# Cross-attention of a decoder layer: two score banks in place of three, two banks for the softmax sums, stack reads in six DMAs in place of twelve

## The chip, the cores and the metric

The kernel runs on one core of a Trainium2 chip. The metric is the device time of one execution in microseconds (us). The kernel before takes 2713.39 us, the median of three runs.

## The reference

One decoder layer over x of shape 16 x 256 x 512 in fp32: windowed self-attention with rotary embedding (16 heads), a cross-attention, and a mixture in which 16 router columns each pick their top tokens. Only the cross-attention matters here:

```python
def _L0_xattn_ref(q, k, v, gamma):      # q = layernorm(x), k = v = ctx_2048, all (16, 256, 512)
    h = 8                               # heads of 32 rows each
    qh, kh, vh = (t.reshape(B, h, 32, 512) for t in (q, k, v))
    qk = jnp.einsum('bhdq,bhdl->bhql', qh, kh) / sqrt(32)
    sm = jax.nn.softmax(qk, axis=-1)
    ret = jnp.einsum('bhql,bhdl->bhdq', sm, vh)
    return gamma * ret.reshape(B, 256, 512)
x = x + _L0_xattn_ref(_layernorm(x), ctx, ctx, gamma)
```

## The kernel before, in words

Three stages follow each other: self-attention, `cross_attention`, `expert_mix`. The change touches `cross_attention` alone. It works on 32 tiles of 128 rows; a tile holds 4 heads of 32 rows. Each engine has a queue of its own, written out by hand; the engines meet through semaphores only.

Operands are split into a high and a low part (`qp`, `kp`). They are written to DRAM scratch (`sq`, `sk`) and read back as stacks of 96 partitions per head (`qst`, `kst`), so that one matmul sums the products of the parts. `read_stacks` does this on SyncE's queue (SP): two halves of two heads, six DMAs each.

A tile has 4 steps (`c` or `h` = 0 to 3) of 4 turns (`i`, `q`). In a turn TensorE issues:

- `scores`, line 784: for a tile 6 steps ahead, 128 queries x 512 keys into one of three PSUM banks `SC`. VectorE's `maximum` (line 930) reduces the bank to one negated maximum a row (`nmx`). `scores` waits for the maximum three scores back.
- `transposed_scores`, line 793: keys x queries of the present tile, with the row maxima as two further rows, into one of two banks `ST`. ScalarE's `exps` (line 870) turns it into probabilities `prt`. It waits for the exponential two back, and at the first turn of a tile for the maxima's rows.

In turn 1 of each step comes `weigh` (line 804, values times probabilities, four column groups packed), at the end of steps 0 and 2 comes `sums` (line 814, the softmax denominators, of `prt` pairs that GpSimd has added), and in step 2 `max_transposes` (line 821) turns the next tile's maxima into rows. Those go through ScalarE (`mhi`, line 891), VectorE (`mlo`, line 935) and two DMAs of `max_rows` (line 714) into `qst`.

The denominators stand in one bank `SU`. ScalarE takes the logarithm (line 881) and the exponential of its negative (line 885), VectorE makes one Newton step (lines 940 and 945) and multiplies the output (line 952); GpSimd adds the residual (line 758); VectorE takes the statistics (lines 957 and 961). Where these small pieces of work stand among exps and maxima is given by a table `WORK` for each of the two engines: (step, turn), the function, and which tile relative to the present one.

Of the kernel before, what the change touches and what calls it, by code (L numbers as in the profile page):

```python
# [5 lines left out]
F32 = mybir.dt.float32  # L6
# [3 lines left out]
ALU = mybir.AluOpType  # L10
ACT = mybir.ActivationFunctionType
AX = mybir.AxisListType

P = 128
# [3 lines left out]
CB = D // P  # L18
# [574 lines left out]
def cross_attention(nc, x1, ctx_in, ctx_t, gamma, sq, sk, mv2, mv3, x2, cst):  # L593
# [4 lines left out]
    with ctx:  # L598
# [3 lines left out]
        def pb(name):  # L602
            return ctx.enter_context(nc.psum_tensor(name, [P, 512], F32))

        def sem(name):
            return ctx.enter_context(nc.semaphore(name))

        PARTS = 3
        KS = PARTS * XD
        KM = KS + 2  # L610
        AHEAD = 6
        RING = 6
        STACKS = 3
# [11 lines left out]
        qst = [sb(f"qst{i}", [P, XPT, D], F32R) for i in range(STACKS)]  # L625
        kst = [sb(f"kst{i}", [P, XPT, D], F32R) for i in range(STACKS)]
        vt = sb("vt", [P, 3, CB, P], F32)
        prt = [sb(f"xprt{i}", [P, XPT, D], F32) for i in range(RING)]
        nmx = sb("xnmx", [P, 2, XPT * CB], F32)
        mhi = sb("xmhi", [XPT * CB, P], F32R)  # L630
        mlo = sb("xmlo", [XPT * CB, P], F32R)
        ones = sb("xones", [P, XD], F32)
        osb = [sb(f"xosb{i}", [P, D], F32) for i in range(2)]
        rin = sb("xrin", [P, D], F32)
        onm = sb("xonm", [P, D], F32)
        bn = sb("bn3", [P, 6], F32)
        SC = [pb(f"xsc{i}") for i in range(3)]
        ST = [pb(f"xst{i}") for i in range(2)]
        MX = pb("xmx")
        OB = pb("xob")  # L640
        SU = pb("xsu")

        s_shift = sem("x_shift")
        s_gam, s_step = sem("x_gam"), sem("x_step")
# [2 lines left out]
        s_qn, s_qhi, s_qlo = sem("x_qn"), sem("x_qhi"), sem("x_qlo")  # L647
        s_khi, s_klo = sem("x_khi"), sem("x_klo")
        s_qw, s_kw = sem("x_qw"), sem("x_kw")
        s_st = [[sem(f"x_st{i}{k}") for k in range(2)] for i in range(STACKS)]  # L650
        s_row = [sem(f"x_row{i}") for i in range(STACKS)]
        s_ones = sem("x_ones")
        s_sc, s_mx = sem("x_sc"), sem("x_mx")
# [5 lines left out]
        s_log, s_inv, s_new = sem("x_log"), sem("x_inv"), sem("x_new")  # L659
# [11 lines left out]
        @block.sync  # L671
        def _(sp):
            sp.dma_start(gam[:, :], gamma.rearrange("(a b) -> a b", a=1).broadcast_to([P, 1])).then_inc(s_gam, 16)

            def load_x(m):
                sp.dma_start(x2[:, m, :], x1v[m // 2, m % 2]).then_inc(s_xi[m % 6], 16)

            def load_context(m):
                if m >= 4:
                    sp.wait_ge(s_klo, m - 3)  # L680
                sp.dma_start(cin[:, m % 4, :], cv[m]).then_inc(s_ci[m % 4], 16)

            def load_values(m):
                if m >= 3:
                    sp.wait_ge(s_pv, CB * (m - 2))
                sp.dma_start(vt[:, m % 3, :, :], ctx_t[m]).then_inc(s_vt[m % 3], 16)

            def write_queries(m):
                sp.wait_ge(s_qlo, m + 1)
                sp.dma_start(sq[m % 2].rearrange("h p d -> p h d"), qp[m % 2][:, :, :].bitcast(F32)).then_inc(s_qw, 16)  # L690

            def write_keys(m):
                sp.wait_ge(s_klo, m + 1)
                sp.dma_start(sk[m % 2].rearrange("h p d -> p h d"), kp[m % 2][:, :, :].bitcast(F32)).then_inc(s_kw, 16)

            def read_stacks(m):
                sp.wait_ge(s_qw, 16 * m + 16)
                sp.wait_ge(s_kw, 16 * m + 16)
                if m >= STACKS:
                    sp.wait_ge(s_ts, 16 * (m - STACKS) + 16)  # L700
                qv = sq[m % 2].rearrange("h (j r) d -> h r j d", j=XPT)
                kv = sk[m % 2].rearrange("h (j r) d -> h r j d", j=XPT)
                for k in range(2):
                    heads, here = slice(2 * k, 2 * k + 2), s_st[m % STACKS][k]
                    for c in range(PARTS):
                        rows = slice(c, KS, PARTS)
                        sp.dma_start(qst[m % STACKS][rows, heads, :].bitcast(F32), qv[c // 2][:, heads, :]).then_inc(here, 16)
                        sp.dma_start(kst[m % STACKS][rows, heads, :].bitcast(F32), kv[c % 2][:, heads, :]).then_inc(here, 16)

            def max_rows(m):  # L710
                for k, (part, here) in enumerate(((mhi, s_mhi), (mlo, s_mlo))):
                    sp.wait_ge(here, m + 1)
                    row = qst[m % STACKS][KS + k:KS + k + 1, :, :].rearrange("o h (q n) -> o (h q) n", n=P)
                    sp.dma_start(row.bitcast(F32), part[:, :].bitcast(F32)).then_inc(s_row[m % STACKS], 16)

            for m in range(4):
                load_x(m)
                load_context(m)
            load_x(4)
            for n in range(-3, TILES):  # L720
                if tile(n + 2):
                    read_stacks(n + 2)
                if tile(n + 3):
                    write_queries(n + 3)
                    write_keys(n + 3)
                if tile(n + 2):
                    load_values(n + 2)
                if n >= 0 and tile(n + 4):
                    load_context(n + 4)
                if n >= 0 and tile(n + 5):  # L730
                    sp.wait_ge(s_qn, n + 2)
                    load_x(n + 5)
                if tile(n + 1):
                    max_rows(n + 1)
# [42 lines left out]
        def _(pe):  # L777
            def scores(g, q):
                m, h = g // CB, g % CB
                if h % 2 == 0 and q == 0:  # L780
                    pe.wait_ge(s_st[m % STACKS][h // 2], 16 * 2 * PARTS * (m // STACKS + 1))
                if 4 * g + q >= 3:
                    pe.wait_ge(s_mx, 4 * g + q - 2)
                nc.tensor.matmul(SC[(4 * g + q) % 3][:, :], qst[m % STACKS][0:KS, h, q * P:(q + 1) * P],  # L784
                                 kst[m % STACKS][0:KS, h, :], start=True, stop=True).then_inc(s_sc, 1)

            def transposed_scores(s, h):
# [19 lines left out]

            def sums(n, k):
                pe.wait_ge(s_add, XPT * (2 * n + k + 1))
                if k == 0:  # L810
                    pe.wait_ge(s_on, n)
                for h in range(XPT):
                    rows = slice(XD * h, XD * (h + 1))
                    last = nc.tensor.matmul(SU[rows, :], ones[:, :], prt[(CB * n + 2 * k) % RING][:, h, :],
                                            start=(k == 0), stop=(k == 1))
                last.then_inc(s_su, 1)

# [20 lines left out]
        def _(act):  # L838
# [39 lines left out]
            def log_of_sums(n):  # L878
                act.wait_ge(s_su, 2 * n + 2)
                act.wait_ge(s_new, 2 * n)  # L880
                nc.scalar.activation(rin[:, :], SU[:, :], ACT.Ln).then_inc(s_log, 1)

            def inverse_of_sums(n):
                act.wait_ge(s_log, n + 1)
# [2 lines left out]
            def max_round(n):  # L887
                act.wait_ge(s_mt, n + 1)
                if n >= 1:
                    act.wait_ge(s_row[(n - 1) % STACKS], 32 * ((n - 1) // STACKS + 1))  # L890
                nc.scalar.activation(mhi[:, :], MX[0:XPT * CB, 0:P], ACT.Copy).then_inc(s_mhi, 1)

            WORK = {(0, 0): ((k_round, 3),), (0, 2): ((output_evac, -1),), (1, 1): ((normed, 4),), (1, 3): ((q_round, 4),),
                    (2, 2): ((max_round, 1),), (3, 0): ((log_of_sums, -1),), (3, 1): ((inverse_of_sums, -1),)}

            for s in range(FIRST, LAST):
                n, c = s // CB, s % CB
# [8 lines left out]
        def _(dve):  # L906
# [17 lines left out]
            def maximum(g, q):  # L924
                m, h = g // CB, g % CB
                dve.wait_ge(s_sc, 4 * g + q + 1)
                if h == 0 and q == 0 and m >= 2:
                    dve.wait_ge(s_mt, m - 1)
                k = CB * h + q
                nc.vector.tensor_reduce(nmx[:, m % 2, k:k + 1], SC[(4 * g + q) % 3][:, :], AX.X, ALU.max,  # L930
                                        negate=True).then_inc(s_mx, 1)

            def max_rest(n):
# [3 lines left out]

            def newton(n):
                dve.wait_ge(s_inv, n + 1)
                nc.vector.scalar_tensor_tensor(SU[:, :], SU[:, :], -1.0, rin[:, :],  # L940
                                               ALU.mult, ALU.mult).then_inc(s_new, 1)

            def newton_end(n):
                dve.wait_ge(s_new, 2 * n + 1)
                nc.vector.scalar_tensor_tensor(SU[:, :], SU[:, :], 2.0, rin[:, :],
                                               ALU.add, ALU.mult).then_inc(s_new, 1)

            def output(n):
                dve.wait_ge(s_new, 2 * n + 2)
                dve.wait_ge(s_oe, n + 1)  # L950
                dve.wait_ge(s_x2, n)
                nc.vector.tensor_tensor(onm[:, :], osb[n % 2][:, :], SU[:, :], ALU.mult).then_inc(s_on, 1)

            def statistics(n):
                dve.wait_ge(s_x2, n + 1)
# [3 lines left out]
            def mean_and_variance(n):  # L959
                dve.wait_ge(s_bn, 2 * n + 1)  # L960
                nc.vector.bn_aggr(mv3[:, n, :], bn[:, :]).then_inc(s_bn, 1)

            WORK = {(0, 0): ((output, -2),), (0, 2): ((statistics, -3),), (1, 0): ((mean_and_variance, -3),),
                    (2, 2): ((max_rest, 1),), (3, 2): ((newton, -1),), (3, 3): ((newton_end, -1),)}

            for s in range(FIRST, LAST):
                n, c = s // CB, s % CB
# [465 lines left out]
```

## Time and profile before

| | |
|---|---|
| median of 3 runs | 2713.39 us (2711.3 to 2716.83) |
| the profiled execution | 2711.3 us |
| its span, first to last instruction | 2709.6 us |
| TensorE busy in the span | 95% |
| VectorE, ScalarE, GpSimd busy | 66%, 36%, 32% |
| cross-attention's matmuls | from 1979.6 us to about 2505 us of the span |

The profile comes from one execution of its own. "Busy" of TensorE is modelled, since matmuls overlap. A timeline row gives start, duration, engine, line, operation, output and inputs, the count of instructions merged into it, and in brackets the idle time ahead of it with what released it. PEld is the weight load that belongs to a matmul.

### The profile page before, as it was taken

Reading aid. Unit: us, or ns where it says so; the run is one execution under the profiler, and the core shown is the slowest. Engines: PE = TensorE matmul, PEld = TensorE weight load, DVE = VectorE, ACT = ScalarE, POOL = GpSimd, SP = SyncE. Lnnn points to the kernel's source line nnn. Section 1 sums busy time; section 2 is a strip of 40 time slices with the busy share of each in tenths; the row PEclk is TensorE's granted clock in tenths of the full one; section 3 lists DMA queues with packets and bytes.
Section 4 is the critical chain, followed back from the end, with each engine's and each line's share of the span. In section 5 each row is a group of like instructions: output and inputs, shape, how many; then the busy total and the mean of one; then the engine's idle time right before and its main releaser. Section 6 shows DMA issues by size and latency. Waiting matters only on the chain. (4 is left out here: it accounts for less than half of the span.)

```text
span 2709.6 us, 37385 instructions
## 1 busy us (share of the span) xinstructions
PE 2570.5 (95%) x12936; PEld 1916.2 (71%) x12936; DVE 1784.2 (66%) x3705; ACT 967.2 (36%) x2435; POOL 861.6 (32%) x698
## 2 busy tenths in 40 slices
PE   6999999999999999999999999999769999999794
PEld 5788888888888888888888888888634444443683
DVE  5777776565566556556655666666558878876657
ACT  2322223322222332222233222222247777776220
POOL 3211112321112232111123211111148888887000
PEclk9999999999999999999999999999969999999897
DMA  3122233221221222122122212210166676662003
GB/s 117 63 78 94 99 119 117 86 78 63 94 87 70 86 86 78 63 93 95 63 86 86 78 63 87 97 67 32 70 214 216 217 228 211 221 221 74 21 1 124
DMA packets 170153, 280.61 MB, mean 104 GB/s; under 512 B 15089, under 2 KB 81649, under 8 KB 169969
## 3 DMA queue, kind: packets, MB, share of 16 engines
q1 hardware_dynamic: 169968, 278.23, 30.5%
q8 instruction: 107, 1.75, 0.3%
q14 instruction: 78, 0.63, 0.1%
HBM read 185.37 MB, written 92.27 MB: 102 GB/s over the span
## 5 line engine op out<-in xcount | busy, mean ns | idle before, releaser
L324 PE MATMUL pj<-xnt,whi 128*128 128x512 f32 x2048 | 706.7, 407 | 5.5 <-DVE xnt L558 5.5
L417 ACT ACTIVATE pr<-sc,nmx 128x128 f32<-128x128 f32 (+1 forms) x512 | 210.6, 416 | 929.0 <-DVE nmx L503 929.0
L269 POOL TENSOR_TENSOR qt<-rot,swp 128x512 f32<-128x512 f32 x128 | 166.0, 1297 | 1109.6 <-DVE swp L483 1109.6
L324 PEld LDWEIGHTS pj<-xnt,whi 128*128 128x128 f32 x2048 | 387.5, 189 | 98.2 <-DVE xnt L558 6.1
L930 DVE TENSOR_REDUCE xnmx<-xsc 128x1 f32<-128x512 f32 x512 | 333.3, 682 | 105.3 <-PE xsc L784 105.0
L324 PE MATMUL pj<-xnt,wlo 128*128 128x512 f32 x1024 | 400.2, 391 | 0.0
L321 PE MATMUL pj<-whi,xnt 128*128 128x512 f32 x1024 | 352.9, 406 | 4.0 <-issue 4.0
L754 POOL TENSOR_TENSOR xprt<-xprt 128x512 f32<-128x512 f32 x256 | 320.8, 1283 | 72.4 <-PE xob L804 72.4
L870 ACT ACTIVATE xprt<-xst 128x512 f32<-128x512 f32 x512 | 290.7, 595 | 129.3 <-PE xst L793 127.8
L481 DVE TENSOR_TENSOR rot<-pj,trig 128x512 f32<-128x512 f32 x256 | 176.7, 690 | 213.2 <-PE pj L324 213.2
L269 POOL TENSOR_TENSOR kt<-rot,swp 128x512 f32<-128x512 f32 x128 | 164.9, 1288 | 306.6 <-DVE swp L483 306.5
L512 DVE TENSOR_SCALAR pr<-pr,rinv 128x128 f32<-128x128 f32 (+1 forms) x512 | 253.6, 536 | 9.0
L784 PE MATMUL xsc<-kst,qst 96*128 96x512 f32 x512 | 228.2, 453 | 30.3 <-DMA kst<-sk_scratch 30.3
L503 DVE TENSOR_REDUCE nmx<-sc 128x1 f32<-128x128 f32 (+1 forms) x512 | 158.5, 351 | 145.9 <-PE sc L358 141.4
L784 PEld LDWEIGHTS xsc<-kst,qst 96*128 96x128 f32 x512 | 99.7, 195 | 200.2 <-DVE xnmx L930 128.4
L321 PEld LDWEIGHTS pj<-whi,xnt 128*128 128x128 f32 x1024 | 193.4, 189 | 50.3 <-issue 4.3
L793 PE MATMUL xst<-qst,kst 98*128 98x512 f32 x512 | 211.8, 416 | 17.5 <-DMA qst<-xmlo 15.2
L324 PEld LDWEIGHTS pj<-xnt,wlo 128*128 128x128 f32 x1024 | 194.9, 190 | 34.6
L345 PE MATMUL pj<-whi,ohi 128*128 128x512 f32 x512 | 212.5, 415 | 1.4 <-DVE olo L517 1.4
L491 DVE TENSOR_TENSOR xio<-pj,xio 128x512 f32<-128x512 f32 x128 | 88.5, 692 | 180.4 <-PE pj L345 180.4
L345 PE MATMUL pj<-whi,olo 128*128 128x512 f32 x512 | 201.6, 394 | 0.0
L321 PE MATMUL pj<-wlo,xnt 128*128 128x512 f32 x512 | 199.8, 390 | 0.0
(183 smaller groups left out, 4226.1 us busy)
## 6 DMA issues: line engine op xcount, KB each, us to landing
xnt<-xt_scratch SPq DMA_DIRECT2D x48, 1024.0 KB, 7.1
x_scratch<-xio SPq DMA_DIRECT2D x64, 512.0 KB, 3.6
xio<-x_scratch SPq DMA_DIRECT2D x48, 512.0 KB, 4.1
qst<-sq_scratch SPq DMA_DIRECT2D x192, 128.0 KB, 2.5
kst<-sk_scratch SPq DMA_DIRECT2D x192, 128.0 KB, 2.6
raw<-in_w_all_dram SPq DMA_DIRECT2D x64, 256.0 KB, 4.6
xt_scratch<-xnt SPq DMA_DIRECT2D x16, 1024.0 KB, 8.9
sq_scratch<-qp SPq DMA_DIRECT2D x32, 512.0 KB, 3.4
```

Source lines behind the costliest of these rows:

```text
L269: nc.gpsimd.tensor_tensor(qk["QK".index(kind)][h][:, :, :].rearrange("p b n -> p (b n)"), rot[r % 2][:, :], swp[r % 2][:, :], ALU.add).the ...
L321: last = nc.tensor.matmul(bank[:, :], moving[:, i * P:(i + 1) * P], wpart[:, w, :], start=(k == 0), stop=(k == 3 * CB - 1))
L324: last = nc.tensor.matmul(bank[:, :], wpart[:, w, i * HD:(i + 1) * HD], moving, start=(k == 0), stop=(k == 3 * CB - 1))
L345: last = nc.tensor.matmul(PJ[n % 3][:, :], o[:, h, tok], w[:, CH_O + h, :], start=(h == 0 and k == 0), stop=(h == HG - 1 and k == 2))
L417: nc.scalar.activation(pr[:, a % 4, lo:hi], SC[a % 2][:, lo:hi], ACT.Exp, bias=nmx[:, a % 4, t:t + 1], accum_out=rsum[:, a % 4, t:t + 1]). ...
L481: nc.vector.tensor_tensor(ro, bank, table(slice(0, P), q), ALU.mult)
L512: nc.vector.tensor_scalar(pr[:, a % 4, lo:hi], pr[:, a % 4, lo:hi], rinv[:, a % 4, t:t + 1], None, ALU.mult).then_inc(s_pr, 1)
L754: nc.gpsimd.tensor_tensor(a[:, h, :], a[:, h, :], b[:, h, :], ALU.add).then_inc(s_add, 1)
L784: nc.tensor.matmul(SC[(4 * g + q) % 3][:, :], qst[m % STACKS][0:KS, h, q * P:(q + 1) * P], kst[m % STACKS][0:KS, h, :], start=True, stop=T ...
L793: nc.tensor.matmul(ST[h % 2][:, :], kst[n % STACKS][0:KM, h, c * P:(c + 1) * P], qst[n % STACKS][0:KM, h, :], start=True, stop=True).then_ ...
L870: nc.scalar.activation(prt[s % RING][:, h, :], ST[h % 2][:, :], ACT.Exp).then_inc(s_exp, 1)
L930: nc.vector.tensor_reduce(nmx[:, m % 2, k:k + 1], SC[(4 * g + q) % 3][:, :], AX.X, ALU.max, negate=True).then_inc(s_mx, 1)
```

## The change

Of PSUM's eight banks, `SC` has two in place of three and `SU` two in place of one. `scores` waits for the maximum two scores back. `read_stacks` reads all four heads of a part in one DMA: six DMAs of twice the size for a tile, with one semaphore for the whole stack. `sums` of a tile waits for the output of the tile two back. In ScalarE's table the inverse (line 885) goes from turn 1 to turn 2 of step 3. In VectorE's table the two Newton operations leave turns 2 and 3 of step 3 for turns 1 and 3 of step 0 of the next tile, the output goes from (0, 0) to (1, 1), the statistics from (0, 2) to (0, 0), and their aggregation from (1, 0) to (0, 2).

```diff
-        SC = [pb(f"xsc{i}") for i in range(3)]
+        SC = [pb(f"xsc{i}") for i in range(2)]
-        SU = pb("xsu")
+        SU = [pb(f"xsu{i}") for i in range(2)]
...
-        s_st = [[sem(f"x_st{i}{k}") for k in range(2)] for i in range(STACKS)]
+        s_st = [sem(f"x_st{i}") for i in range(STACKS)]
...
-                for k in range(2):
-                    heads, here = slice(2 * k, 2 * k + 2), s_st[m % STACKS][k]
-                    for c in range(PARTS):
-                        rows = slice(c, KS, PARTS)
-                        sp.dma_start(qst[m % STACKS][rows, heads, :].bitcast(F32), qv[c // 2][:, heads, :]).then_inc(here, 16)
-                        sp.dma_start(kst[m % STACKS][rows, heads, :].bitcast(F32), kv[c % 2][:, heads, :]).then_inc(here, 16)
+                for c in range(PARTS):
+                    rows = slice(c, KS, PARTS)
+                    sp.dma_start(qst[m % STACKS][rows, :, :].bitcast(F32), qv[c // 2]).then_inc(s_st[m % STACKS], 16)
+                    sp.dma_start(kst[m % STACKS][rows, :, :].bitcast(F32), kv[c % 2]).then_inc(s_st[m % STACKS], 16)
...
-                if h % 2 == 0 and q == 0:
-                    pe.wait_ge(s_st[m % STACKS][h // 2], 16 * 2 * PARTS * (m // STACKS + 1))
-                if 4 * g + q >= 3:
-                    pe.wait_ge(s_mx, 4 * g + q - 2)
-                nc.tensor.matmul(SC[(4 * g + q) % 3][:, :], qst[m % STACKS][0:KS, h, q * P:(q + 1) * P],
+                if h == 0 and q == 0:
+                    pe.wait_ge(s_st[m % STACKS], 16 * 2 * PARTS * (m // STACKS + 1))
+                if 4 * g + q >= 2:
+                    pe.wait_ge(s_mx, 4 * g + q - 1)
+                nc.tensor.matmul(SC[q % 2][:, :], qst[m % STACKS][0:KS, h, q * P:(q + 1) * P],
...
-                if k == 0:
-                    pe.wait_ge(s_on, n)
+                if k == 0 and n >= 2:
+                    pe.wait_ge(s_on, n - 1)
...
-                    (2, 2): ((max_round, 1),), (3, 0): ((log_of_sums, -1),), (3, 1): ((inverse_of_sums, -1),)}
+                    (2, 2): ((max_round, 1),), (3, 0): ((log_of_sums, -1),), (3, 2): ((inverse_of_sums, -1),)}
...
-            WORK = {(0, 0): ((output, -2),), (0, 2): ((statistics, -3),), (1, 0): ((mean_and_variance, -3),),
-                    (2, 2): ((max_rest, 1),), (3, 2): ((newton, -1),), (3, 3): ((newton_end, -1),)}
+            WORK = {(0, 0): ((statistics, -3),), (0, 1): ((newton, -2),), (0, 2): ((mean_and_variance, -3),),
+                    (0, 3): ((newton_end, -2),), (1, 1): ((output, -2),), (2, 2): ((max_rest, 1),)}
```

## Rows read from the trace of the kernel before

**Rows 1.** Windows: us, busy (x) of PE, PEld, DVE, ACT, POOL; clock, DMA share, GB/s.

```profile
2016.60:2216.70 200.10, 193.87 (x1035) 81.04 (x1033) 158.83 (x273) 152.60 (x293) 172.29 (x138) 1.00 0.69 220
```

**Rows 2.** Timeline of TensorE's matmuls, pieces of one tile, and fifteen tiles later.

```profile
2203.35 0.50 PE L784 MATMUL xsc<-kst,qst 96*128 96x512 f32 x1
2203.69 0.40 PE L793 MATMUL xst<-qst,kst 98*128 98x512 f32 x1
2203.92 0.40 PE L784 MATMUL xsc<-kst,qst 96*128 96x512 f32 x1
2204.16 0.40 PE L793 MATMUL xst<-qst,kst 98*128 98x512 f32 x1
2204.39 0.39 PE L784 MATMUL xsc<-kst,qst 96*128 96x512 f32 x1
2205.44 0.50 PE L793 MATMUL xst<-qst,kst 98*128 98x512 f32 x1 [0.67 <-DMA qst<-xmlo]
...
2207.33 0.50 PE L784 MATMUL xsc<-kst,qst 96*128 96x512 f32 x1
...
2211.57 0.50 PE L784 MATMUL xsc<-kst,qst 96*128 96x512 f32 x1
...
2212.61 0.39 PE L784 MATMUL xsc<-kst,qst 96*128 96x512 f32 x1
2212.99 0.50 PE L793 MATMUL xst<-qst,kst 98*128 98x512 f32 x1
...
2215.01 0.50 PE L784 MATMUL xsc<-kst,qst 96*128 96x512 f32 x1
...
2219.25 0.50 PE L784 MATMUL xsc<-kst,qst 96*128 96x512 f32 x1
...
2441.31 0.47 PE L793 MATMUL xst<-qst,kst 98*128 98x512 f32 x1
```

**Rows 3.** Waits over those fifteen tiles: who waited for whom, us, times, longest.

```profile
PEld xst L793 <- DMA qst<-xmlo: 13.0, 14, 2.3
PEld xst L793 <- ACT xprt L870: 9.1, 30, 0.4
```

**Rows 4.** Timeline of VectorE: first scores of the stage, and a tile's unpacked stretch.

```profile
1980.47 9.66 DVE L930 TENSOR_REDUCE xnmx<-xsc 128x1 f32<-128x512 f32 x16 [14.04 <-PE xsc L784]
...
2212.11 2.48 DVE L930 TENSOR_REDUCE xnmx<-xsc 128x1 f32<-128x512 f32 x4 [0.77 <-PE xsc L784]
```

**Rows 5.** Timeline of TensorE's weight loads at the stage's first scores.

```profile
1979.63 0.93 PEld L784 LDWEIGHTS xsc<-kst,qst 96*128 96x128 f32 x3 [27.51 <-issue]
1981.21 0.29 PEld L784 LDWEIGHTS xsc<-kst,qst 96*128 96x128 f32 x1 [0.65 <-DVE xnmx L930]
```

**Rows 6.** Timeline of ScalarE around the inverse.

```profile
2203.45 0.64 ACT L885 ACTIVATE xrin<-xrin 128x512 f32<-128x512 f32 x1
2204.12 1.08 ACT L870 ACTIVATE xprt<-xst 128x512 f32<-128x512 f32 x2
```

**Rows 7.** Timeline of SyncE's queue: a maxima DMA, first and last stack read.

```profile
2201.26 0.59 SPq L714 DMA_DIRECT2D qst<-xmlo  x1
2204.64 0.61 SPq L707 DMA_DIRECT2D qst<-sq_scratch  x1
...
2211.68 0.60 SPq L708 DMA_DIRECT2D kst<-sk_scratch  x1
```

**Rows 8.** DMA issues from 2100 to 2400 us: count, KB each, median us to landing.

```profile
kst<-sk_scratch SPq DMA_DIRECT2D x114, 128.0 KB, 2.7
...
qst<-xmlo SPq DMA_DIRECT2D x19, 8.0 KB, 3.4
```

**Rows 9.** Windows: the twelve stack reads of one tile, columns as in rows 1.

```profile
2204.60:2212.30 7.70, 7.03 (x39) 2.96 (x39) 6.90 (x13) 5.65 (x11) 5.73 (x6) 1.00 0.57 165
```

**Rows 10.** Timeline of TensorE: second tile's first scores, first transposition of maxima.

```profile
1992.32 1.22 PE L784 MATMUL xsc<-kst,qst 96*128 96x512 f32 x2 [3.14 <-DMA kst<-sk_scratch]
1993.34 0.41 PE L821 MATMUL xmx<-ident,xnmx 128*16 128x128 f32 x1
```

More of the change, by code:

```diff
@@ L809, in sums @@
                 pe.wait_ge(s_add, XPT * (2 * n + k + 1))
-                if k == 0:
-                    pe.wait_ge(s_on, n)
+                if k == 0 and n >= 2:
+                    pe.wait_ge(s_on, n - 1)
                 for h in range(XPT):
                     rows = slice(XD * h, XD * (h + 1))
-                    last = nc.tensor.matmul(SU[rows, :], ones[:, :], prt[(CB * n + 2 * k) % RING][:, h, :],
+                    last = nc.tensor.matmul(SU[n % 2][rows, :], ones[:, :], prt[(CB * n + 2 * k) % RING][:, h, :],
                                             start=(k == 0), stop=(k == 1))
@@ L880, in log_of_sums @@
                 act.wait_ge(s_new, 2 * n)
-                nc.scalar.activation(rin[:, :], SU[:, :], ACT.Ln).then_inc(s_log, 1)
+                nc.scalar.activation(rin[:, :], SU[n % 2][:, :], ACT.Ln).then_inc(s_log, 1)
             def inverse_of_sums(n):
@@ L929, in maximum @@
                 k = CB * h + q
-                nc.vector.tensor_reduce(nmx[:, m % 2, k:k + 1], SC[(4 * g + q) % 3][:, :], AX.X, ALU.max,
+                nc.vector.tensor_reduce(nmx[:, m % 2, k:k + 1], SC[q % 2][:, :], AX.X, ALU.max,
                                         negate=True).then_inc(s_mx, 1)
@@ L939, in newton @@
                 dve.wait_ge(s_inv, n + 1)
-                nc.vector.scalar_tensor_tensor(SU[:, :], SU[:, :], -1.0, rin[:, :],
+                nc.vector.scalar_tensor_tensor(SU[n % 2][:, :], SU[n % 2][:, :], -1.0, rin[:, :],
                                                ALU.mult, ALU.mult).then_inc(s_new, 1)
@@ L944, in newton_end @@
                 dve.wait_ge(s_new, 2 * n + 1)
-                nc.vector.scalar_tensor_tensor(SU[:, :], SU[:, :], 2.0, rin[:, :],
+                nc.vector.scalar_tensor_tensor(SU[n % 2][:, :], SU[n % 2][:, :], 2.0, rin[:, :],
                                                ALU.add, ALU.mult).then_inc(s_new, 1)
@@ L951, in output @@
                 dve.wait_ge(s_x2, n)
-                nc.vector.tensor_tensor(onm[:, :], osb[n % 2][:, :], SU[:, :], ALU.mult).then_inc(s_on, 1)
+                nc.vector.tensor_tensor(onm[:, :], osb[n % 2][:, :], SU[n % 2][:, :], ALU.mult).then_inc(s_on, 1)
             def statistics(n):
```

## The prediction

> **What bounds the kernel now.** The page comes first; it gives the span in which the change touches one stage of three. The windows then show what is tight in it: in 200.1 us TensorE is busy for 193.87 at full granted clock, VectorE for 158.83, ScalarE for 152.60 and GpSimd for 172.29 [rows 1]. So the order of TensorE's queue sets the pace, and everything else matters as far as it makes TensorE wait.
>
> The timeline of one tile shows how [rows 2]. The first transposed score of a tile starts at 2205.44, that of fifteen tiles later at 2441.31: (2441.31 - 2205.44) / 15 = 15.72 us a tile. How much of this is waiting? A score and a transposed score follow each other by 0.23 us (2203.69 to 2203.92), and by 0.34 when the first of them comes after a packed group, since its weight load then can't be hidden (2203.35 to 2203.69). A packed group (`weigh` or `sums`) ends most half-steps. A half-step with its group takes 2.12: 2207.33 to 2211.57 is two of them in 4.24, and 2215.01 to 2219.25 again two in 4.24. In these four, VectorE and ScalarE have the second of the group to catch up. Between lie two stretches in which four scores and four transposed scores follow each other without a group in the middle. I call them A (2211.57 to 2215.01, 3.44 us, with the transposition of maxima) and B (2203.35 to 2207.33, 3.98 us; it runs over a tile's start).
>
> In A one transposed score is 0.38 behind its score in place of 0.23 (2212.61 to 2212.99), and pays 0.11 more for its uncovered load: 0.26 of waiting, and 3.18 without it. In B the tile's first transposed score comes 1.05 after the score (2204.39 to 2205.44), where 0.23 is enough, and again 0.11 for the load: 0.93, and 3.05 without it. A tile without waits is 4 x 2.12 + 3.18 + 3.05 = 14.71 us; so the mean tile waits 15.72 - 14.71 = 1.01, and if A takes its 0.26, B waits 0.75 on average. The waits name the causes: over fifteen tiles 13.0 us for the DMA of `xmlo`, 9.1 for exps [rows 3]. This 1.01 is all that any rearrangement can win while TensorE's work stays.
>
> **The change, part by part.** *Two score banks.* The price is a loop: a score's load, the time until its maximum starts, the maximum, and the release of the bank. Load to maximum is 0.54 at full clock: the score that opens A loads at 2211.57, its maximum starts at 2212.11 [rows 2, 4]. A run of four maxima takes 2.48 and one of sixteen 9.66, so they follow each other by 0.60 and one lasts 0.68 [rows 4]. The release is short: the first maximum ends at 1980.47 + 0.68 = 1981.15, and the load that waited for it starts at 1981.21, 0.06 later [rows 4, 5]. Take A's first load as 0. Its maximum runs from 0.54 to 1.22, and with two banks the third score loads at 1.28. Its matmul stood at 1.04 up to now (2211.57 to 2212.61), with its load hidden. A matmul whose load was held back is followed after 0.34 and not 0.23, so the next one starts at 1.62 in place of 1.27: 0.35 late. The second maximum starts at 1.14 and ends at 1.82, the fourth score loads at 1.88 and is followed at 2.22, where 1.62 + 0.23 + 0.23 = 2.08 would have been its natural time: 0.14 more. So 0.49 in A and, by the same steps, 0.49 in B. In the packed half-steps nothing is lost: the third score there comes 2.12 after the first, and its bank is free at 1.28.
>
> In A these 0.49 take the place of the 0.26 that it waits now, as the exponentials gain the same time. A becomes 3.18 + 0.49 = 3.67.
>
> *VectorE's table.* The five moved operations are the same as before, and cost TensorE nothing as long as VectorE reaches the first maximum of A and B at once. It does: it is idle for 0.77 ahead of A's [rows 4], and in B two Newton operations leave the places where they would now hold a bank. Were they to stay, each 0.60 would come on top in B; without the cover of the following packed group the statistics and the first Newton operation would cost as much. The two `SU` banks only take a wait out of `sums` that was already met; zero, since nothing waits there in the rows.
>
> *The inverse on ScalarE.* It leaves its place ahead of the third exponential of step 3, where it started at 2203.45 while ScalarE waited anyhow [rows 6], for one between the third and the fourth. The third still starts at 2204.12, which is 0.77 after B's first load. A pair of exponentials takes 1.08, so the next operation can follow after 0.48: inverse at 1.25. It lasts 0.64 and, overlapped like the others (0.60 of 0.68 above), lets the fourth exponential start some 0.53 later, at 1.78, and end at 2.38. The tile's second transposed score waits for it, loads at about 2.43, and is followed 0.44 later by the packed group: 2.87. Without this wait it would start at 2.22 and the group at 2.55. So 0.32 more in B; at least nothing (if something else holds B longer), at most the whole 0.53.
>
> *The stack reads.* Twelve issues from 2204.64 to 2211.68 are 0.64 apart [rows 7]; six fewer free SyncE's queue 3.8 us earlier. The transfers of values, context and x that now go out just ahead of the maxima's rows then go out earlier, and the `xmlo` DMA, 3.4 us to landing [rows 8] after its issue at 2201.26 [rows 7], meets an emptier queue. Also B now brings its tile's start 0.35 later. I take the `xmlo` wait as gone: from -0.75 in B, if that were all of it, to 0. So B becomes 3.05 + 0.49 + 0.32 = 3.86.
>
> Against it, the scores of a tile now wait for all of its stack. Bytes: 12 x 128 KB = 1.57 MB. During the stack reads the DMA engines moved 165 GB/s at a share of 0.57 [rows 9], so about 290 at a full share (an estimate); 1.57 MB need 5.4 us. One read lands after 2.7 us [rows 8], of which 128 KB at that rate take 0.45, so the last lands about 2.25 + 5.4 = 7.7 us after the first issue. It is needed at the third score of A. The first issue is 0.48 behind the last transposed score of a tile (2204.16 to 2204.64), thus 1.29 into B; A's third score is at 3.86 + 4.24 + 1.28 = 9.38. That leaves 8.1 - 7.7 = 0.4 us to spare: nothing lost, but narrowly. The Trainium skill, "DMA: Bandwidth & Descriptors", section on the anatomy of one DMA (fitted on GpSimd's path), has about 2.0 us fixed and 436 GB/s after that. By the page the last of six, issued 3.2 us after the first, would land 2.6 us later, at 5.8, with 2.3 us to spare. The row of this kernel shows a slower movement, so the cover is thinner than by the page.
>
> *The start.* Before the first exponential only scores run. The first load to the first maximum takes 1980.47 - 1979.63 = 0.84 at the lower clock [rows 4, 5], so two banks give (0.84 + 0.68 + 0.06) / 2 = 0.79 a score in place of 0.60, and the whole stack is awaited, about 1.4 us longer. Up to the transposition of maxima (1993.34 [rows 10]) that makes 1.4 + 16 x 0.19 = 4.4, of which 3.1 vanish in the wait for the second tile's stack that stands there now [rows 10]: 1.3 late. But six issues fewer are ahead of the maxima's DMAs (-3.8). Between these I take -1.
>
> **The sum.** A tile: 8.48 + 3.67 + 3.86 = 16.01 against 15.72: +0.29, some 30 times +8.7; the start -1. From the profiled execution's 2711.3 us: 2719.0. That execution lies 2.1 us under the median of the runs shown, so 2721 on the median's level.
>
> **The rivals.** *Faster: banks free in time.* If the third score did not really have to wait (a release or a start of the maximum that is 0.3 quicker at this place), only ScalarE's wait stays and the `xmlo` wait is gone: 14.71 + 0.26 + 0.32 = 15.29, 0.43 less a tile, -13 - 1, thus about 2699. It decides at a loop of 1.04 us in place of 1.28. Against it: 0.54, 0.68 and 0.06 are all rows. The skill's "Perfetto Trace Analysis", section on DMA optimizations, holds that larger DMAs use the bandwidth better and may be the main gain. By this rule the change should win at the stack reads, which is this rival's other half; but the stage is not bound by bytes, and the same section says that a split lets some work start sooner.
>
> *No change.* The new waits exist, but of the inverse's 0.32 nothing shows, since the fourth exponential has time, or B's old wait was larger. Then 15.69 a tile and 2711 to 2716 in all.
>
> *Late stacks.* The last read lands more than 0.4 us later than reckoned. Each further microsecond is paid on every tile, because nothing on TensorE overtakes: one microsecond late is +30, thus 2751. For it: rival traffic and issues that took longer; against: the queue is free of other reads then.
>
> *The reorder does nothing and the `xmlo` wait stays.* Then B waits for both, and at most 0.75 x 30 = 22 us come on top: 2743.
>
> **Chances.** Forecast's mechanism 0.58, within it most of the weight over 2719; faster 0.12; no change 0.12; late stacks or a staying `xmlo` wait 0.18. The sum's own error is about 0.1 us a tile, 3 us in all, and a measurement tells about 0.2% (5.4 us) from no change; a part of the forecast's weight, 0.11, thus falls to "within 0.2%". Slower 0.65, same 0.23, faster 0.12. The range reaches from the upper part of the faster side to 1 us of late stacks: 2707 to 2747; the likeliest case alone has 2715 to 2728.
>
> **What would show it.** In the profile after: weight loads of line 784 that wait for `xnmx` inside A and B, about 0.2 to 0.35 us each, twice a stretch; a transposed score at B's end that waits for line 870 with line 885 right ahead of the fourth exponential; no `xmlo` wait of line 793 or a small one; six stack reads 0.64 apart and SyncE's queue idle ahead of `xmhi`; no wait for `kst` or `qst` from scratch at step 2. A tile should measure 16.0 us. The prediction is wrong if loads of line 784 wait for the stack DMAs, if a third score follows its first by 1.04 as now, or if GpSimd's sums hold `sums`.

## Result, and the profile after

The changed kernel takes 2738.35 us, the median of four runs (2734.95 to 2745.65), beside 2714.22 us before: ratio 1.0087, interval 1.0068 to 1.0105. It is slower, by 24 us, inside the range (2707 to 2747), but 17 above the value that I named. The profiled execution took 2744.02 us around a span of 2742.3.

The first lines of the profile's page after (its first transposed score comes 2.7 us later than before, at 2003.28; the rest is in the tiles):

```profile
span 2742.3 us, 37159 instructions
## 1 busy us (share of the span) xinstructions
PE 2591.8 (95%) x12936; PEld 1920.3 (70%) x12936; DVE 1794.3 (65%) x3705; ACT 968.3 (35%) x2435; POOL 861.5 (31%) x698
```

TensorE's timeline after: a stretch B, a stretch A, and the fourth and 31st transposition of maxima:

```profile
2233.70 0.50 PE L782 MATMUL xsc<-kst,qst 96*128 96x512 f32 x1
...
2237.57 0.50 PE L782 MATMUL xsc<-kst,qst 96*128 96x512 f32 x1
...
2241.83 0.50 PE L782 MATMUL xsc<-kst,qst 96*128 96x512 f32 x1
...
2243.82 0.50 PE L782 MATMUL xsc<-kst,qst 96*128 96x512 f32 x1 [0.79 <-DMA kst<-sk_scratch]
...
2246.06 0.50 PE L782 MATMUL xsc<-kst,qst 96*128 96x512 f32 x1
...
2046.53 0.27 PE L819 MATMUL xmx<-ident,xnmx 128*16 128x128 f32 x1
...
2497.55 0.27 PE L819 MATMUL xmx<-ident,xnmx 128*16 128x128 f32 x1
```

A tile takes (2497.55 - 2046.53) / 27 = 16.70 us; by the same two rows of the kernel before (2039.65 and 2465.07) it was 15.76. The two packed half-steps from 2237.57 to 2241.83 still take 4.26. B is 3.87 here, and 3.86 on average over the tiles, against 3.78. A is 4.23 here and 4.34 on average, against 3.44. So nearly all of the 0.95 us a tile is in A. (All averages of this kind are counted over the whole stage's timeline, of which a few rows are shown. Averages of A and B here and below are taken over the stage's 31 tiles without the first three and last two, from one score after a packed group to the next.)

The weight loads say what held them:

```profile
2234.98 0.19 PEld L782 LDWEIGHTS xsc<-kst,qst 96*128 96x128 f32 x1 [0.51 <-DVE xnmx L928]
...
2235.58 0.19 PEld L782 LDWEIGHTS xsc<-kst,qst 96*128 96x128 f32 x1 [0.20 <-DVE xnmx L928]
2236.13 0.19 PEld L791 LDWEIGHTS xst<-qst,kst 98*128 98x128 f32 x1 [0.37 <-ACT xprt L868]
...
2243.82 0.19 PEld L782 LDWEIGHTS xsc<-kst,qst 96*128 96x128 f32 x1 [1.22 <-DMA kst<-sk_scratch]
```

In B the third score loads at 1.28 after the first (2233.70 to 2234.98), the fourth at 1.88, and the second transposed score at 2.43: to the hundredth where the prediction had them. In A the third score waits for the stack and loads at 1.99, 0.71 late; A is only 0.58 longer than 3.65, as the wait of the fourth score is then covered.

The waits over the stage, from 2010 to 2480 us, and the DMA issues from 2100 to 2400:

```profile
PEld xsc L782 <- DMA kst<-sk_scratch: 32.4, 27, 2.7
...
PE xsc L782 <- DMA kst<-sk_scratch: 20.5, 26, 2.3
...
PEld xst L791 <- ACT xprt L868: 9.8, 27, 0.4
```

```profile
qst<-sq_scratch SPq DMA_DIRECT2D x54, 256.0 KB, 4.1
kst<-sk_scratch SPq DMA_DIRECT2D x54, 256.0 KB, 4.7
sq_scratch<-qp SPq DMA_DIRECT2D x18, 512.0 KB, 6.2
...
qst<-xmlo SPq DMA_DIRECT2D x17, 8.0 KB, 1.9
```

No wait for `xmlo` is left, and its DMA lands in 1.9 us where it took 3.4 [rows 8]. In its place stands a wait for `kst` on nearly every tile. SyncE's queue shows why `xmlo` has a free way, and when the reads went out:

```profile
2235.01 0.61 SPq L705 DMA_DIRECT2D qst<-sq_scratch  x1
...
2238.23 0.60 SPq L706 DMA_DIRECT2D kst<-sk_scratch  x1
...
2242.64 0.62 SPq L676 DMA_DIRECT2D x<-x_scratch  x1
2247.60 0.56 SPq L712 DMA_DIRECT2D qst<-xmhi  x1
```

From 2243.3 to 2247.6 the queue is idle. The last stack read is usable at 2243.82, 8.81 us after the first issue at 2235.01. The prediction had 7.7, and 8.1 as the moment from which it costs.

The medians of 4.1 and 4.7 us to landing hide an order. Over the stage the first of a tile's six reads lands in 3.3 us (median), the next in 3.8, 4.2, 4.7 and 5.1, and the sixth, issued 3.22 us after the first, in 5.5.

One thing more is in A. On two of the 25 tiles whose records are complete, the granted clock fell after the wait (see e3), and there A is 7.30 and 6.23; on the other 23 it is 4.11. So of the 0.69 us above 3.65, some 0.46 are the wait for the stack on tiles at full clock, and two tiles bring the rest.

### The profile page after: what moved, and what is told of

Read it like the earlier page. It is cut to its first block and busy times, and to the rows that moved or that the text cites. A ratio compares the mean times of both kernels' runs of the same rounds, so it can differ in the third digit from the quotient of the medians.

```text
span 2742.3 us, 37159 instructions
## 1 busy us (share of the span) xinstructions
PE 2591.8 (95%) x12936; PEld 1920.3 (70%) x12936; DVE 1794.3 (65%) x3705; ACT 968.3 (35%) x2435; POOL 861.5 (31%) x698
## 5 line engine op out<-in xcount | busy, mean ns | idle before, releaser
L782 PE MATMUL xsc<-kst,qst 96*128 96x512 f32 x512 | 241.6, 476 | 56.7 <-DMA kst<-sk_scratch 51.7
```

Of the source, the lines that this page charges most:

```text
L782: nc.tensor.matmul(SC[q % 2][:, :], qst[m % STACKS][0:KS, h, q * P:(q + 1) * P], kst[m % STACKS][0:KS, h, :], start=True, stop=True).then_ ...
```

## The experiments

Nine kernels in three groups (the first four, the next four, the last). Each median stands beside that of the kernel before on the same chip (2714.05, 2714.38 and 2714.64 us). "Tile" is the mean distance of transpositions of maxima, by the same rows as above.

| kernel | median us | ratio, interval | tile | A | B |
|---|---|---|---|---|---|
| before | - | - | 15.76 | 3.44 | 3.78 |
| changed | 2738.35 | 1.0087 (1.0068 to 1.0105) | 16.70 | 4.34 | 3.86 |
| e1 split reads | 2724.52 | 1.0036 (1.0023 to 1.0048) | 16.07 | 3.65 | 3.89 |
| e2 merged reads alone | 2746.37 | 1.0118 (1.0104 to 1.0131) | 17.03 | 4.99 | 3.38 |
| e3 inverse back | 2747.44 | 1.0117 (1.0101 to 1.0132) | 16.87 | 4.75 | 3.54 |
| e4 writes held | 2733.29 | 1.0070 (1.0058 to 1.0083) | 16.37 | 4.00 | 3.86 |
| e5 two banks, old tables | 2735.17 | 1.0081 (1.0065 to 1.0097) | 16.55 | 3.65 | 4.14 |
| e6 rows of maxima first | 2700.35 | 0.9952 (0.9938 to 0.9966) | 15.38 | 3.44 | 3.39 |
| e7 split reads, one wait | 2799.42 | 1.0321 (1.0301 to 1.0342) | 18.70 | 5.91 | 3.86 |
| e8 split reads, inverse back | 2717.89 | 1.0016 (1.0006 to 1.0026) | 15.88 | 3.65 | 3.71 |
| e9 two banks, best order | 2715.13 | 0.9998 (0.9986 to 1.0010) | 15.74 | 3.65 | 3.55 |

(For B of e2, e3 and e7 the value of nearly all tiles stands; a few matmul records are missing there.)

**e1, split reads.** The changed kernel with the reads and the two semaphores of before:

```diff
-                for c in range(PARTS):
-                    rows = slice(c, KS, PARTS)
-                    sp.dma_start(qst[m % STACKS][rows, :, :].bitcast(F32), qv[c // 2]).then_inc(s_st[m % STACKS], 16)
-                    sp.dma_start(kst[m % STACKS][rows, :, :].bitcast(F32), kv[c % 2]).then_inc(s_st[m % STACKS], 16)
+                for k in range(2):
+                    heads, here = slice(2 * k, 2 * k + 2), s_st[m % STACKS][k]
+                    for c in range(PARTS):
+                        rows = slice(c, KS, PARTS)
+                        sp.dma_start(qst[m % STACKS][rows, heads, :].bitcast(F32), qv[c // 2][:, heads, :]).then_inc(here, 16)
+                        sp.dma_start(kst[m % STACKS][rows, heads, :].bitcast(F32), kv[c % 2][:, heads, :]).then_inc(here, 16)
...
-                if h == 0 and q == 0:
-                    pe.wait_ge(s_st[m % STACKS], 16 * 2 * PARTS * (m // STACKS + 1))
+                if h % 2 == 0 and q == 0:
+                    pe.wait_ge(s_st[m % STACKS][h // 2], 16 * 2 * PARTS * (m // STACKS + 1))
```

> The changed kernel with its stack reads put back to twelve DMAs and two semaphores a tile; banks and tables as changed. Theory A (the whole-stack wait costs what my sum lacked: stretch A took 4.34 us a tile where 3.65 is its length without that wait, 0.69 x 30 = 21 us, and the start came about 3 us later): A goes back to 3.67, B to 3.86 or up to 0.3 more where the maxima's rows land late again, a tile 16.0 to 16.2, so 9 to 15 us above the kernel before and 12 to 20 below the changed one (about 2722 to 2729 when before has 2714). Theory B (two banks cost more than reckoned and the stack wait only takes the place of a bank wait): A stays near 4.3, no gain over the changed kernel.

A fell to 3.65 on every tile, the tile to 16.07, the time to 10.5 us above the kernel before and about 14 below the changed one. Theory A holds: with each half awaited by itself, the wait of A is gone. This kernel is the prediction's sum without late stacks.

**e2, merged reads alone.** The reverse edit on the kernel before: six reads and one semaphore, three banks, old tables.

> The kernel before with the six merged stack reads alone; three score banks, old tables. Theory A (last read lands 8.85 us after the first issue, as in the changed kernel): A's third score is due 1.29 + 8.67 - 2.58 = about 7.4 us after the first issue, so it waits some 1.4 us; the maxima's rows land in 1.9 us and B falls from 3.78 to 3.39. Tile 8.48 + 3.39 + 4.6 = 16.4 to 16.5 against 15.75, +0.7 x 30 = about +20 us. Theory B (merged reads are harmless where banks are free; fewer DMAs help the maxima's rows): B falls by 0.4 and A stays 3.44, -12 us.

Both halves of theory A came, B 3.38 and a later A, and A came worse than expected: 4.99 in place of 4.6, and +32 us in place of +20. So this one part of the change costs more alone than the whole change. On the 19 of 25 tiles at full clock A is 4.57, as expected; the miss is on tiles where the granted clock fell (5.75 to 6.90), which e3 explains.

**e3, inverse back.** The changed kernel with

```diff
-                    (2, 2): ((max_round, 1),), (3, 0): ((log_of_sums, -1),), (3, 2): ((inverse_of_sums, -1),)}
+                    (2, 2): ((max_round, 1),), (3, 0): ((log_of_sums, -1),), (3, 1): ((inverse_of_sums, -1),)}
```

> The changed kernel with the inverse alone put back to turn 1 of step 3. Its price in B was 0.32 us. Theory A (the stack reads start after a tile's last transposed score, so the time to their landing is a chain of its own and a shorter B only lengthens A's wait): B 3.54, A 4.34 + 0.2 to 0.3, gain only on the tiles whose stack is in time, 0 to -4 us against the changed kernel. Theory B (waits add up): B 3.54, A 4.34, -0.32 x 30 = -10 us.

B is 3.54 as both had it, but A is 4.75, 0.41 longer, and the kernel is not faster than the changed one: 2747 beside 2738. Theory B falls. Theory A gave no loss either, and here its ratio lies above the changed kernel's, with intervals that just touch (1.0101 to 1.0132, 1.0068 to 1.0105). The trace shows what it had left out. The windows of e3 around one late stack (columns as in rows 1), the score that waited, and the packed group (`weigh`) behind it:

```profile
2120.00:2128.00 8.00, 7.93 (x43) 3.27 (x41) 7.08 (x13) 6.50 (x13) 6.74 (x6) 1.00 0.46 117
2128.00:2132.20 4.20, 2.55 (x15) 0.87 (x13) 2.88 (x5) 3.32 (x6) 2.73 (x3) 0.98 1.03 299
2132.20:2138.80 6.60, 6.60 (x21) 2.82 (x25) 2.59 (x5) 2.38 (x5) 4.69 (x4) 0.50 0.50 189
```

```profile
2132.16 0.80 PE L782 MATMUL xsc<-kst,qst 96*128 96x512 f32 x1 [1.65 <-DMA kst<-sk_scratch]
...
2134.38 1.94 PE L802 MATMUL xob<-xprt,vt 128*32 128x512 f32 x8
```

TensorE stood idle for 1.65 us and the granted clock fell from 1.00 to 0.50, from 2.4 to 1.2 GHz, for the next 6.6 us: the packed group takes 1.94 where it takes 1.06. That tile's A was 7.0 us. The clock records of the stage after its warm start show 6 such falls in e3, 7 in e2, 3 in the changed kernel, 12 in e7, and none in the others or before. On the tiles at full clock A is 4.37 in e3 beside 4.11 in the changed kernel: +0.26, just what theory A had for the later stack. The rest of A's growth stands on the tiles where the clock fell.

Each fall stands at the end of a wait for a stack of 1.14 to 2.96 us, or less than two microseconds behind it. But the length of the idle does not decide it: the changed kernel has one of 1.42 us at 2194.12 and e7 one of 2.63 at 2030.02 with a clock of 1.00 behind them, and so has the kernel before, whose longest wait for `xmlo` goes by at full clock:

```profile
2379.53 0.50 PE L793 MATMUL xst<-qst,kst 98*128 98x512 f32 x1 [1.87 <-DMA qst<-xmlo]
```

```profile
2379.50:2384.00 4.50, 4.47 (x25) 1.87 (x26) 3.43 (x6) 3.26 (x6) 3.14 (x3) 1.00 0.62 194
```

More and longer idles went with more falls; what decides on a single one stays open.

**e4, writes held.** The changed kernel with SyncE waiting for the stack ahead of the writes:

```diff
                     read_stacks(n + 2)
+                    sp.wait_ge(s_st[(n + 2) % STACKS], 16 * 2 * PARTS * ((n + 2) // STACKS + 1))
```

> The changed kernel with one wait more on SyncE's queue: it waits for the whole stack to land before it issues the next tile's query and key writes, values, context and x. Theory A1 (the reads land late because the writes issued right behind them share the DMA engines: 6.2 us to landing for writes, 4.1 to 4.7 for reads that had 2.5 to 2.7): the last read lands 7.7 us after the first issue in place of 8.85, A falls to 3.7 to 3.9, a tile to 16.0 to 16.2, 12 to 18 us below the changed kernel, unless the maxima's rows now land behind the loads again. Theory A2 (six reads of 256 KB need that long by themselves): A stays 4.3 and nothing is gained.

Half of each. SyncE's first read and the load that waited for the last, in e4:

```profile
2230.12 0.60 SPq L705 DMA_DIRECT2D qst<-sq_scratch  x1
```

```profile
2238.80 0.19 PEld L783 LDWEIGHTS xsc<-kst,qst 96*128 96x128 f32 x1 [1.08 <-DMA kst<-sk_scratch]
```

Over the 29 tiles the third score of A loads 8.2 to 9.3 us after the first read's issue, median 8.5; in the changed kernel 8.15 to 10.3, median 8.75. A went from 4.34 to 4.00, not to 3.7. So the reads by themselves need longer than my 7.7, and the writes behind them add a quarter of a microsecond at the median and the worst tiles. No clock falls are left, and that is the larger part of the gain in A: on the changed kernel's tiles at full clock A was 4.11 already. On time the two kernels' intervals overlap, so a gain is not shown.

As no write is issued behind the reads here, e4 also shows where the 8.6 us of one stack go (windows, columns as in rows 1):

```profile
2230.12:2232.12 2.00, 1.94 (x8) 0.88 (x12) 2.00 (x4) 2.00 (x6) 2.00 (x3) 1.00 0.24 72
2232.12:2237.12 5.00, 5.00 (x33) 1.85 (x26) 4.73 (x9) 3.76 (x8) 3.13 (x3) 1.00 1.03 277
2237.12:2238.80 1.68, 1.05 (x5) 0.50 (x5) 1.41 (x3) 1.33 (x4) 1.67 (x2) 1.00 0.14 33
```

For two microseconds the engines are mostly idle, for five they are full at 277 GB/s, and when nearly all bytes (1.53 of 1.57 MB) are over, 1.68 us pass before the score can load. At 277 GB/s all bytes take 5.7 us; 2.9 us of the 8.6 are not movement of bytes.

**e5, two banks with the old tables.** The kernel before with `SC` of two banks, the index `% 2`, and the wait `s_mx, 4 * g + q - 1`; one `SU`, twelve reads.

> The kernel before with two score banks in place of three and nothing else (one bank for the sums, twelve reads, old tables). Same loop as before (0.54 + 0.68 + 0.06): A 3.66. In B the two Newton operations stand between the maxima: the second maximum ends at 2.42, the fourth score loads at 2.48 and B becomes 4.14, and the output ahead of the fourth maximum costs 0.28 more in the packed half-step behind it. Theory A (tables matter because two banks bind VectorE's order to TensorE's): tile 8.44 + 3.66 + 4.14 + 0.28 = 16.5, some 0.45 above the split-reads kernel's 16.07, +23 us on the kernel before. Theory B (the tables are indifferent): as the split-reads kernel, +10 us.

A 3.65, B 4.14, tile 16.55: theory A to 0.05. The fourth score's load in B, held by the second maximum, which stands behind a Newton operation:

```profile
2212.94 0.19 PEld L784 LDWEIGHTS xsc<-kst,qst 96*128 96x128 f32 x1 [0.80 <-DVE xnmx L930]
```

Against e1 this is 0.48 us a tile (16.55 to 16.07), but e1 also has the later inverse, which costs. The clean partner is e8, with reads and ScalarE's table as here, on the same chip: VectorE's new table together with the second `SU` bank gives 17.3 us (2735.17 to 2717.89), 0.67 us a tile. No run separates the two.

Of the two Newton operations only one is felt in B: 4.14 beside 3.55 in e9, 0.59. The packed half-steps take 2.19 on average, beside 2.13 in e8 and e9.

**e6, rows of maxima first.** The kernel before with one change of order in SyncE's loop:

```diff
+                if tile(n + 1):
+                    max_rows(n + 1)
                 if n >= 0 and tile(n + 4):
                     load_context(n + 4)
                 if n >= 0 and tile(n + 5):
                     sp.wait_ge(s_qn, n + 2)
                     load_x(n + 5)
-                if tile(n + 1):
-                    max_rows(n + 1)
```

> The kernel before with one change of order on SyncE's queue: the two DMAs of maxima's rows are issued ahead of the loads of context and x and not behind them. B alternates now between 3.38 and about 4.0, mean 3.78, by the landing of xmlo (3.4 us to landing behind those loads, 1.9 where nothing was ahead of it). Theory A: xmlo lands in 2.5 us or less, B goes to 3.38 on nearly all tiles, -0.4 x 30 = -12 us, faster than both kernels. Theory B: the loads, issued later, delay the stack reads behind them, or the xmhi wait blocks the queue; no gain.

Theory A holds. B is 3.39, where it had jumped between 3.38 and 5.2, and every tile takes 15.4. Its DMA issues from 2100 to 2400 us:

```profile
cin<-in_ctx_in_dram SPq DMA_DIRECT2D x20, 256.0 KB, 2.9
x<-x_scratch SPq DMA_DIRECT2D x20, 256.0 KB, 3.0
...
qst<-xmlo SPq DMA_DIRECT2D x20, 8.0 KB, 2.5
```

It takes 2700.35 us, 14 less than the kernel before, and beats both kernels.

**e7, split reads with one wait.** e1, but a tile's scores wait for both halves:

```diff
-                if h % 2 == 0 and q == 0:
-                    pe.wait_ge(s_st[m % STACKS][h // 2], 16 * 2 * PARTS * (m // STACKS + 1))
+                if h == 0 and q == 0:
+                    for k in range(2):
+                        pe.wait_ge(s_st[m % STACKS][k], 16 * 2 * PARTS * (m // STACKS + 1))
```

> The split-reads kernel (twelve reads, two banks, new tables) with the wait of the changed kernel: a tile's scores wait for both halves. Theory A (what costs is the whole-stack wait, and twelve issues make it later still): the last read is issued 7.04 after the first and lands 2.6 later, 9.6, where A's third score is due at 8.2; A 3.65 + 1.5 = 5.1, tile 17.4 or more, about 2765 us or above with clock drops. Theory B (large DMAs are what is slow, small ones are not): as the split-reads kernel, 2724.

A 5.91 and 2799 us, 75 us above e1, whose DMAs are the same. Theory B is out: what costs is that the first score waits for the last read, not the size of a DMA. Given the one wait, six large reads (2738) are far better than twelve small ones. A is 0.8 above expectation: on the 13 of 25 tiles without a clock fall it is 5.35, 0.25 above the 5.1, and the other 12 (5.69 to 7.40) bring the rest. The wait in e7, from 2010 to 2480 us:

```profile
PE xsc L785 <- DMA kst<-sk_scratch: 51.9, 26, 2.6
```

**e8, split reads and the inverse back.** e1 with e3's edit.

> The split-reads kernel with the inverse back at turn 1 of step 3. Here no stack is late, so if the inverse's place costs 0.32 in B, it shows: Theory A: B 3.54 where the maxima's rows land in time, up to 0.2 more on average as they now bind again; tile 15.75 to 15.9, 2715 to 2720 us, 5 to 9 below the split-reads kernel. Theory B (another wait takes its place entirely): 2724.

6.6 us below e1, as theory A had it: B is 3.54 on more than half of the tiles and 3.7 to 4.3 on the rest, mean 3.71, since the maxima's rows bind again.

**e9, two banks in their best order.** e8 with e6's edit.

> Split reads, inverse back at turn 1, and the maxima's rows issued ahead of context and x, with the two score banks and the tables of the changed kernel. Only the loop of two banks is left of the change, and neither stacks nor xmlo bind. Theory A (the waits of a stretch are a maximum of chains and the bank loop is 0.49 in each of A and B): A 3.65, B 3.54 on every tile, tile 8.44 + 3.65 + 3.54 = 15.65, 0.1 below the kernel before's 15.76 and 0.27 above the 15.38 of three banks with the same order of DMAs: 2708 to 2713 us, beside 2700 there. Theory B (the row DMAs of maxima were not what kept B at 3.71 in the kernel with the inverse back): B stays 3.7, 2716 or more.

A and B came as theory A had them (3.65, 3.55) and are steady; the tile is 15.74, 0.1 above the expected 15.65. That 0.1 is in the expectation: it took 8.44 for the four packed half-steps, but they take 2.13 each on average, in e6 and e8 as here, 8.5 in all (8.5 + 3.65 + 3.55 = 15.7). The time is that of the kernel before (0.9998, 0.9986 to 1.0010), above the 2708 to 2713 expected, and 15 us above e6. Three banks against two, all else in order: 15.38 against 15.74 us a tile, which is 11 us over 30 tiles. (The profiled execution of e9 was the fastest of twelve, 2710.48, and lies 10 us above e6's 2700.24.)

## Why the prediction came out as it did

*The base and the two score banks.* Right. The loop of 0.54, 0.68 and 0.06 put the loads of B at 1.28 and 1.88, and there they are. A without a late stack was to be 3.67 and is 3.65 (e1, e5, e8, e9).

*The inverse on ScalarE.* Right in place and size: 2.43 foreseen and measured, 0.32 us in B (3.86 against 3.54 in e3, and on most tiles of e8). Putting it back is worth 6.6 us where no stack is late (e8 against e1), and nothing where one is (e3).

*VectorE's table.* Right that it costs nothing as it stands: e8 and e9 have A 3.65 and B 3.54. What the old one would cost in B was put at 0.60 for each Newton operation, 1.20; e5 against e9 shows 0.59 for both. The first holds the second maximum, and with it B's fourth score; the second holds a maximum for which only the next half-step waits. That the second `SU` bank by itself is worth nothing was not tested.

*The `xmlo` wait.* Right: gone, as SyncE's queue empties earlier and B begins its tile later. e1 shows that the second reason nearly suffices: with twelve reads again and `xmlo` landing in 3.2 us (median), B is 3.89.

*The stack reads.* This is the step that failed: "nothing lost, but narrowly". The margin was 8.1 - 7.7 = 0.4 us; the last read came at 8.5 alone (e4) and 8.75 with the writes behind it (medians). The moment from which it costs, 8.1, was right. I had scaled a share of 0.57 at 165 GB/s to 290 GB/s and let nothing share the engines. That scaling was nearly right (277 GB/s in e4, 5.7 us in place of 5.4). The larger miss is the time that is not movement: 2.25 us in the prediction, taken from 128 KB reads, and 2.9 us in e4's windows. Sharing with the writes adds the last quarter of a microsecond.

The rival of late stacks had the right place. Its price of 1 us for 1 us is nearly right at full clock (0.58 for 0.71 above), but it left out that TensorE's clock may fall when the idle grows. It had 0.18 of the chances together with another case, and the forecast without it 0.58: with 0.4 us of margin on an estimate of 7.7 the odds should have been near even. So the measured 2738 lies in the range, and in the forecast direction, partly by this rival's cost and not by the forecast's mechanism alone, which gives 2724 (e1). The range's top was not consistent either: 2747 for 1 us of late stacks, where the rival itself has 2751.

The Trainium skill, "DMA: Bandwidth & Descriptors", section on the anatomy of one DMA, has about 2.0 us plus the bytes at 436 GB/s, fitted on another path. By it one 256 KB read would take 2.6 us and, if each went by itself, the last of six would land 5.8 us after the first issue. The trace does not agree for this queue: the first read, with the engines free, took 3.3 us, the sixth 5.5, and the last landed at 8.75. The Trainium skill's "Perfetto Trace Analysis", section on DMA optimizations, has both rules, that larger DMAs use bandwidth better and that a split lets work start sooner. The second shows in e1 against the changed kernel (14 us). In e7 against the changed kernel the fewer, larger DMAs win by 61 us where one wait stands for all, but by their issues and not by bandwidth: the last of twelve is issued 7.05 us after the first and lands at 9.9, the last of six at 3.22 and 8.75.

*The start.* Wrong in sign, small in size. From the first stack read to the first transposed score it took 27.0 us before (1973.59 to 2000.58 in its timeline) and 28.2 after (1975.09 to 2003.28): +1.2 where I had -1.

*The sum.* Without late stacks: +0.29 a tile foreseen, +0.31 in e1 (16.07 against 15.76), 2721 foreseen and 2724.5 measured. The chain of waits in A and B was right there by its steps, not by luck. The profiled execution's 32.7 us of span: 0.95 x 30 = 28 in the tiles, 1.2 at the start, 1.5 lost ahead of the stage in that execution (the stage's first DMA is issued at 1959.23, not 1957.74); about 2 are not accounted for. The median's 24 is less than the profile's. The four executions lie 10.7 us apart, but so do the fifteen of the kernel before beside e5 to e8 (2710.01 to 2720.66), so this spread says nothing about the stacks.

## What to carry to other kernels

Replay one period of the bounding queue with the rows' latencies: for bank loops that was good to a few hundredths of a microsecond. For a wait on the last of several DMAs it is not (7.7 reckoned, 8.0 to 10.3 measured); a margin smaller than the spread of landings is no cover, so keep the semaphore split where the first user needs only the first half. Where every wait is the maximum of several chains, shortening one may only lengthen another (e3), and the cheapest gain may be the order of issues: here the two small DMAs that the queue waits for, put ahead of two large ones that nobody awaits.

## What the runs showed of the hardware

A wait of TensorE within a warm stretch can cost more than itself: after an idle of 1.65 us in e3 the granted clock was 0.50 over the next 6.6 us, and a packed group took 1.94 us in place of 1.06. It need not: idles of 1.42 us (the changed kernel at 2194), 1.87 (before at 2380) and 2.63 (e7 at 2030) went by at 1.00.

An 8 KB DMA on SyncE's queue took 1.9 us to landing where nothing was on the way (the changed kernel), 2.5 where two 512 KB writes and one 256 KB load (values) had been issued ahead of it (e6), and 3.4 where two more 256 KB loads (context and x) had been (before).

Six 256 KB reads issued 0.64 us apart landed in 3.3 us (the first) to 5.5 us (the sixth), twelve of 128 KB so issued in 2.5 to 2.8, without such a growth. With the engines full these reads moved 277 GB/s (e4), and the last could be used 1.68 us after the window in which they were full.
